# A graph network kernel: each tile of gathered rows fetched once, and copied on the chip to the steps that use it

## What is computed

```python
edge_index = jnp.stack([src, dst])
h = jnp.maximum(_layernorm(x, axis=-1), 0.0)
x = x + _L0_gnn_ref(h, src, dst, L0_gnn_W, L0_gnn_b)              # mean of h[src] over the edges of a node, @ W.T + b
...
x = x + _L1_gnn_ref(h, src, dst, L1_gnn_W_edge, ...)              # mean of relu([h[src], h[dst]] @ W_edge.T), then a linear layer and relu
...
x = x + _L2_gnn_ref(h, edge_index, ...)                           # two graph attention layers, 16 heads of 8
...
x = x + _L3_gnn_ref(h, edge_index, ...)                           # attention by dot products q[dst] * k[src], 2 heads of 64
```

## Time and profile before

| | |
|---|---|
| time, median of 3 runs | 6830.07 us (6825.1 to 6843.93) |
| the profiled execution, its own time | 6823.64 us |
| its span | 6821.9 us |
| mean granted TensorE clock | 0.636 |
| busy shares | PE 49%, PE weight load 42%, DVE 40%, ACT 31%, POOL 50% |
| DMA moved | 564.68 MB, mean 83 GB/s |
| fetches by POOL, L1165 | 3520, busy 3355.5 us |
| chain that ended last, by engine | unknown 48%, DVE 17%, PE 14%, issue 13% |

### The profile page before, as it was taken

The page is one execution under the profiler, slowest core; times in us unless marked ns, Lnnn a source line. Parts: engine busy times, 40 slices in busy tenths (PEclk is TensorE's granted clock), DMA queues, the critical chain, the costliest instruction groups (busy, mean ns, idle before and its releaser), DMA issues.

```text
span 6821.9 us, 113042 instructions
## 1 busy us (share of the span) xinstructions
PE 3345.8 (49%) x30004; PEld 2897.9 (42%) x30005; DVE 2697.0 (40%) x6412; ACT 2103.5 (31%) x6369; POOL 3437.8 (50%) x3641
## 2 busy tenths in 40 slices
PE   1545445444444454454454534444444555555555
PEld 1434334333333343444444534444444455555454
DVE  4222223211111144444444544444445644444445
ACT  1111112222222233444444434444444322222222
POOL 3666664455555525555555355455454444444443
PEclk9565666767776665556555655555666666666666
DMA  4222222222222222222222232222222333333332
GB/s 114 91 87 88 90 85 83 80 74 78 75 76 77 75 56 75 78 78 82 78 78 82 56 83 81 77 78 81 77 77 62 103 97 100 96 98 96 98 95 80
DMA packets 342830, 564.68 MB, mean 83 GB/s; under 512 B 90413, under 2 KB 160957, under 8 KB 342622
## 3 DMA queue, kind: packets, MB, share of 16 engines
q0 software_dynamic: 124288, 289.37, 16.1%
q1 hardware_dynamic: 218354, 273.42, 12.7%
HBM read 490.31 MB, written 72.84 MB: 83 GB/s over the span
## 4 chain that ended last, share of the span: by engine, by line
another core or an unknown queue 48%; DVE 17%; PE 14%; issue 13%; ACT 3%; DVEq 2%; ACTq 1%; POOL 1%; DMA 0%; SPq 0%; POOLq 0%
PE psA L1564 7%; PE psDS L1189 3%; DVE acc L1683 2%; PE psDS L1542 2%; DVE prod L1589 1%; PE psA L1230 1%; DVE lg L1598 1%; DVE seg L1605 1%; DVE lastmax L1615 1%; DVE lastmax L1613 1%; DVE below L1661 1%; DVE V L1670 1%; DVE prod L1396 1%; DVE lastmax L1617 1%
## 5 line engine op out<-in xcount | busy, mean ns | idle before, releaser
L1165 POOL DMA_INDIRECT GT<-table,srcI x3520 | 3355.5, 953 | 3202.6 <-DVE V L1670 1403.7
L1564 PE MATMUL psA<-V,O 128*128 128x144 f32 (+1 forms) x4176 | 988.6, 425 | 10.8 <-ACT psA L1500 5.5
L1189 PE MATMUL psDS<-nodeQ,Ot 128*128 x2816 | 605.7, 390 | 658.3 <-ACT Ot L1181 559.8
L1564 PEld LDWEIGHTS psA<-V,O 128*128 128x128 f32 x4176 | 918.0, 314 | 17.2 <-issue 11.8
L1189 PEld LDWEIGHTS psDS<-nodeQ,Ot 128*128 128x128 f32 x2816 | 544.6, 290 | 696.4 <-issue 691.3
L1519 PE MATMUL psDS<-stageD,Ot 128*128 128x16 bf16 x4224 | 251.4, 173 | 804.2 <-issue 802.9
L1519 PEld LDWEIGHTS psDS<-stageD,Ot 128*128 128x128 bf16 x4224 | 184.3, 102 | 878.2 <-issue 860.4
L1683 DVE TENSOR_TENSOR acc<-acc,psA 128x1296 f32 (+1 forms) x261 | 381.2, 1460 | 413.8 <-remote 349.8
L1661 DVE TENSOR_TENSOR below<-lg,psDS 128x128 f32<-128x128 f32 (+1 forms) x264 | 62.4, 236 | 1157.8 <-remote 1156.6
L1500 ACT COPY psA<-consts 128x1296 f32<-128x1296 f32 (+1 forms) x261 | 315.0, 1207 | 628.4 <-DVE acc L1683 471.9
L1550 PE MATMUL psDS<-newM,Ot 128*128 128x16 bf16 (+1 forms) x6336 | 256.5, 175 | 430.2 <-issue 291.3
(11 more groups left out here) (244 smaller groups left out, 5286.0 us busy)
## 6 DMA issues: line engine op xcount, KB each, us to landing
Ob<-onehots SPq DMA_DIRECT2D x352, 256.0 KB
Ot<-onehots_turned SPq DMA_DIRECT2D x352, 256.0 KB
GT<-table,srcI POOLq DMA_INDIRECT x3520
onehots<-Ob SPq DMA_DIRECT2D x88, 256.0 KB
onehots_turned<-Ot SPq DMA_DIRECT2D x88, 256.0 KB
first<-first_dram SPq DMA_DIRECT2D x176, 64.0 KB
first_dram<-GT SPq DMA_DIRECT2D x18, 384.0 KB, 5.1
table<-nodeQ SPq DMA_DIRECT2D x40, 128.0 KB, 1.9
```

The costliest lines, as they stand in the source:

```text
L1165: eng.indirect_dma_start(out=GT[:, p.k, j, 0:table.shape[1]], out_offset=None, in_=table, in_offset=bass.IndirectOffsetOnAxis(ap=srcI[:, p ...
L1189: ins = eng.matmul(psD[:, j, :], Ot32[:, p.q, j, :], at_block(nodeQ, b[j], D), start=True, stop=True)
L1564: ins = eng.matmul(to, O[:, p.q, j, :], V[:, p.q, j, 0:VW], start=False, stop=j == G - 1, skip_group_check=True)
```

## The change

The first four passes (sum, mlp, gat1, gat2) get their rows in two stages.

- **`fetch_tiles` on POOL** fetches each of the 665 tiles once, in NT = 84 groups of eight, into a ring of 4 x 8 tiles. It is written out, with no hardware loop. From tile group 4 on it first loads from `tiles_over` which step group must have been copied, and waits for that on the new counter `copied`. Behind the fifth fetch of each group it waits for the group before to have landed and raises `landed`. In the gat passes the fourth group also waits for `parted(0)`.
- **`copy_rows` on SP** copies, for each step of a group, its tile from the tile ring to the row ring, which the other engines read as they read `GT` before: it waits for the row ring's release, loads eight slot numbers (`slots_of_steps`) and two needs (`tiles_needed`) into registers, waits for `landed` twice, and issues 4 + 4 DMAs from SBUF to SBUF. `rows_copied` waits for them to land and raises `copied`.
- SP's loads of the next group's one-hot matrices stand between `copy_rows` and `rows_copied` (mlp and gat); in the sum pass both stand ahead of the stores.
- ACT has no `copy_index` in these passes. Both rings share the buffer `rows_of_edges`, whose second part also holds `prod`.
- The setup works out the new index tables: three more loads, one more set of transposes, about ten more vector operations, and a store of the steps' indices to `src_steps`. Some constants move to `Ot32`, and the units begun in the mlp pass move into `acc` (`own_sums`).
- The dot pass keeps `fetch_groups` and `copy_index`; it reads its indices from `srcT`, which SP reloads from `src_steps` at the end of gat2.

The core of the diff, cut:

```diff
-def sweep(eng, n, turn, early=0, late=0):
+def sweep(eng, n, turn, early=0, late=0, tail=0):
...
-    last = (n - early) // RING
+    last = (n - max(early, tail)) // RING
...
-        GT = sb("GT", [P, RING, G, 2 * D])
+        rows_of_edges = sb("rows_of_edges", [P, RING * G * 2 * D + HEADS1 + G * D])
...
+        def fetch_tiles(eng, table, hold=None):
+            tables_stored(eng)
+            to = by_tiles(table.shape[1])[1]
+
+            def has_landed(n):
+                eng.wait_ge(*ring_tiles[n % RING](n // RING, min(G, T - n * G) - 1))
+                eng.sem_inc(landed.sem, 1)
+
+            for n in range(NT):
+                k = n % RING
+                if n >= RING:
+                    eng.wait_ge(*copied(loaded(eng, "over", tiles_over, n - RING, 1, NG - 1, for_waits=True)[0]))
+                    apart(eng)
+                if n == RING - 1 and hold is not None:
+                    eng.wait_ge(*hold(0))
+                for t in range(n * G, min(n * G + G, T)):
+                    eng.indirect_dma_start(
+                        out=to[:, t % (RING * G), :], out_offset=None, in_=table,
+                        in_offset=bass.IndirectOffsetOnAxis(ap=srcT[:, t:t + 1], axis=0),
+                    ).then_inc(ring_tiles[k].sem, 16)
+                    if t % G == G // 2 and n:
+                        has_landed(n - 1)
+            if T % G <= G // 2:
+                has_landed(NT - 2)
+            has_landed(NT - 1)
+
+        def copy_rows(eng, p, w, release):
+            to, of = by_tiles(w)
+            last = isinstance(p.g, int) and p.g == NG - 1
+            eng.wait_ge(*release(p.g - RING))
+            apart(eng)
+            at = loaded(eng, "slots", slots_of_steps, p.g, G, RING * G - 1)
+            need = loaded(eng, "need", tiles_needed, p.g, 2, NT - 1, for_waits=True)
+            parts = [(0, G // 2, need[0]), (G // 2, G, need[1])]
...
+            for a, z, group in parts:
+                eng.wait_ge(*landed(group))
+                apart(eng)
+                for j in range(a, z):
+                    eng.dma_start(to[:, p.k, j, :], of[:, bass.ds(at[j], 1), :].rearrange("p o w -> p (o w)"))\
+                       .then_inc(ring_rows[p.k].sem, 16)
+
+        def rows_copied(eng, p):
+            eng.wait_ge(*ring_rows[p.k](p.i))
+            eng.sem_inc(copied.sem, 1)
...
 # sum pass
-                    fetch_groups(eng, NG, table, sums)
+                    fetch_tiles(eng, table)
...
                     def turn(p):
+                        copy_rows(eng, p, D, sums)
+                        rows_copied(eng, p)
                         eng.wait_ge(*onehot(p.g))
...
-                        if p.has(RING):
-                            copy_index(eng, p.plus(RING))
...
 # mlp pass
-                    sweep(eng, NG, lambda p: load_hots(eng, p, (onehot32,), (turned32,)))
+                    def turn(p):
+                        if p.has(0):
+                            copy_rows(eng, p, D, prodded)
+                        if p.has(1):
+                            load_hots(eng, p.plus(1), (onehot32,), (turned32,))
+                        if p.has(0):
+                            rows_copied(eng, p)
+                    sweep(eng, NG, turn, early=1)
...
 # softmax pass
+                    if gat:
+                        fetch_tiles(eng, table, parted)
+                    else:
+                        fetch_groups(eng, NG, table, values)
...
+                    def turn(p):
+                        if p.has(0):
+                            copy_rows(eng, p, VW, values)
+                        if p.has(1):
+                            load(p.plus(1))
+                        if p.has(0):
+                            rows_copied(eng, p)
...
+                    if to_x == 3:
+                        eng.wait_ge(*landed(NT - 1))
+                        eng.dma_start(srcT[:, :], src_steps).then_inc(src_loaded, 16)
```

More of the change, by code:

```diff
@@ L76, in program @@
     SP_ = SC * P
+    NT = -(-T // G)
     FULL, REST = N // P, N % P
@@ L187, in loaded @@
             eng.load(regs, table[0:1, bass.ds(g * (of or n), n)])
+            if for_waits:
+                if (eng.engine, which, "held") not in reg_sets:
+                    reg_sets[eng.engine, which, "held"] = [eng.alloc_register(f"{which}_held_{j}") for j in range(n)]
+                held = reg_sets[eng.engine, which, "held"]
+                for r, to in zip(regs, held):
+                    eng.reg_alu(to, r, 0, ALU.max)
+                regs = held
             return [eng.snap(r, min_val=0, max_val=most) for r in regs]
@@ L199, in program @@
         noted.per = G
+        ring_tiles = [Count(sem(f"tiles{r}"), G, 16) for r in range(RING)]
+        landed, copied, src_loaded = Count(sem("landed")), Count(sem("copied")), sem("src_loaded")
         ring_rows = [Count(sem(f"rows{r}"), 1, 16 * G) for r in range(RING)]
@@ L370, in _ @@
                     do(eng.tensor_copy, WG[k][:, D:D + 2 * HEADS1], psS[:, 64 * k:64 * k + 2 * HEADS1])
+                eng.wait_ge(tables_turned, TILE_SRC)
+                do(eng.tensor_copy, srcT[:, :], psN[:, 0:SC, :].rearrange("p c s -> p (c s)"))
+                marks["tiles out"] = count
                 eng.wait_ge(fetched, 16 * 2 * SC)
@@ L1171, in copy_index, with tiles_closed @@
+        def rows_copied(eng, p):
+            eng.wait_ge(*ring_rows[p.k](p.i))
+            eng.sem_inc(copied.sem, 1)
+        def tiles_closed():
+            landed.close(NT)
+            copied.close(NG)
+            for k in range(RING):
+                ring_tiles[k].base += 16 * len([t for t in range(T) if t // G % RING == k])
         def copy_index(eng, p):
             if not (isinstance(p.i, int) and p.i <= 0):
-                eng.wait_ge(*ring_rows[p.k](p.i - 1))
+                eng.wait_ge(*ring_tiles[p.k](p.i - 1))
@@ L1346, in _ @@
                     rest_of_units(eng, phase, phase.tensor)
-            close((index, onehot, turned, onehotT, onehot32, sums, counted, added), NG)
+            close((onehot, turned, onehotT, onehot32, sums, counted, added), NG)
+            tiles_closed()
             rows_closed(NG)
@@ L1419, in _ @@
                     rest_of_units(eng, phase, phase.tensor)
-            close((index, onehot32, turned32, toedge, prodded, values, sums, added), NG)
+            close((onehot32, turned32, toedge, prodded, values, sums, added), NG)
+            tiles_closed()
             rows_closed(NG)
@@ L1704, in turn @@
                     def turn(p):
-                        if p.has(RING):
+                        if not gat and p.has(RING):
                             copy_index(eng, p.plus(RING))
@@ L1728, in turn @@
                             act_onehot32(eng, p)
+                    if not gat:
+                        eng.wait_ge(src_loaded, 16)
                     sweep(eng, NG, turn, early=RING, late=1)
```

125 lines of the change are left out of this document (86 added, 39 removed).

## The result

The changed kernel takes 7196.6 us (median of 4 runs, 7184.1 to 7212.5) where the kernel before takes 6828.1: the ratio is 1.0536, with a 95% interval of 1.0509 to 1.0563. The change costs 5.4%. The profiled execution has a span of 7182.4 us against 6821.9. One thing must be known to read what follows: in five of the seven later comparisons the very same kernel before took 4910 to 4920 us (the lower level) and in the other two 6826 and 6832 (the level of this comparison), so kernels are compared only within a level.

What follows compares the result with a forecast made beforehand. It took POOL's fetch stretches, nearly in series with the other engines they slow, as the bound. Fewer fetches −135, starts +45, setup +5, SP's copies +35 gave −50 on 6823.6: 6774, as run median 6780 us; range 6640 to 7500.

Steps and rivals of the forecast that it cites:

- The likeliest case: Whole kernel: fewer fetches outweigh later starts and SP's copies, 6780 us (own range 6690 to 6820), chance 0.36.
- SP becomes the bound: Rival: copy landing not covered, SP's period 14.3 us; sum +220, mlp +53, gats −45 each, 7018 us; chance 0.22.
- P = 14.3: SP's period per group in us if the landing falls outside slow time, in the rival where SP bounds; 0.22.
- signs that were to make the forecast wrong: Sum pass above 12.5 us per group with PE waiting for rows; POOL pauses ending on SP in the gats.
- P = 12.2 us for SP in the sum pass: SP's period per group with copies, landing in slow time; against 11.8 before, +35 us (−49 to +290).
- W: SP's work per group at normal pace, copies, loads, hot matrices and waits: 7.9 us, landing up to 1.9 more.
- s: Time per group in which POOL's fetches slow SP to one instruction per 0.70 us: 4.6 to 6.6 us.
- −45 us for each gat pass: gat1 and gat2: 39 fetches fewer at 1.256 us save 49, 45 counted, taken whole.
- fetches in series with the rest: Gat passes: 10 us of fetches plus some 5 us of free running make the 14.9 us period.
- mlp, −45: mlp pass: the gain from 39 fewer fetches taken whole, since PE suffers there the same way.
- Starts, +45: First four passes: first rows used 22.6 us after the first fetch instead of 11.4, 11.2 later four times.
- The landing of 3.6 us: Copies queued behind fetched rows land in 3.6 instead of 1.9 us; sum-pass period 13.9 us, whole kernel 6930.

Runs made afterwards that it cites:

- e13: Changed kernel with SP counting copies right behind them in mlp and gat, behind the stores in the sum pass; 7217.1 us beside 6825.5 for the kernel before.
- e14: Changed kernel with every second row copy left out (odd steps read old rows); 7185.3 us beside 6825.5 for the kernel before.
- e9: Changed kernel with four of each group's eight copies in the sum pass issued by ACT; 7154.7 us beside 6831.5 for the kernel before.
- e6: Change in the mlp pass alone, sum and both gat passes fetching as before; 6764.0 us beside 6831.5 for the kernel before.
- e16: Changed kernel with POOL in the gat passes also waiting for `values` of the third group behind; 4873.6 us beside 4912.8 for the kernel before.
- e2: Changed kernel with copies counted right behind them in mlp and gat, behind the stores in the sum pass; 5114.8 us beside 4910.0 before.

## Why the prediction was wrong

It forecast 6780 us, faster; measured was slower, 7196.6. The likeliest case was the wrong one of those that it listed. The rival "SP becomes the bound" had the side and the sum pass right (P = 14.3, +220 us) and mlp and the gat passes wrong. Its total is mis-added too: 6830 + 220 + 53 − 90 + 50 is 7063 and not 7018. Both of the signs that were to make the forecast wrong came: a sum pass of over 12.5 us per group with PE waiting for rows, and pauses of POOL that end on SP in the gat passes.

- **The step that failed first: P = 12.2 us for SP in the sum pass**, from a landing that falls into slow time. It doesn't: POOL is released by the count behind the landing, so in 79 of the pass's 88 turns at least nine tenths of the wait for it lay outside of POOL's fetches, and it was added whole, 1.7 us. SP's turn is 14.4 us and the pass +216 us, where the text took +35. The other parts were sized nearly right: W plus landing 7.9 + 1.9 = 9.8 against 10.4 at the lower level, and the slowing 4.0 us of 5.6 x 0.81 = 4.5. But s was taken too narrow: 9.6 us less the 2 to 5 that it names are 4.6 to 7.6 and not 6.6. e13 shows what the landing is worth (119 us of 216) and that the pass is still +110 without it; e14 and e9 show 92 us for half the copies and 57 for moving them to ACT. Whether these gains add wasn't tried; e9 shows another stall by POOL's stretches taking over.
- **The second: −45 us for each gat pass.** They took +101 and +123. The reading of the earlier trace rows, fetches in series with the rest, made the saving whole; it left out that POOL's release would no longer come from V but from SP's count, so that stretches and groups fall out of step. What that costs can be read from the same two profiles, from one `below` of DVE to the next, by how much of POOL's fetching lies between them. Before, 77 of 79 such intervals of gat1 (2600 to 3800 us) have one stretch in them and last 14.8 to 16.0 us. In the changed kernel (2740 to 4020 us) 14 of 77 have none and last 8.4 us (median), 15 have two and last 24.7, so such a pair takes 33.1 us where two groups took 30.0; six have just one and last 14.8 to 18.0, and the rest have parts of stretches. The mean is 16.2 us against 15.0. In e13 (2760 to 4040 us) 36 of 79 have one stretch and last 16.2 us in the median, 13.4 to 18.4. So a stretch of the same length costs the others more at most places than where it fell before. The copies are beside it in all of these intervals, and no run at this level had the old place with copies, so that the place alone is the cause stays argued. Shown is that it isn't SP's number of copies (e14), nor the count behind the loads (e13), nor late rows, nor PE's clock, and that the old form in gat gives the old time (e6).
- **mlp, −45:** right in sign, −85 measured, −68 in e6. It hangs on the count behind the loads: counted ahead of them it is +44 against before (1347 against 1302, e13). 39 fetches of 1.256 us are only 49 us. For the rest there is a term that the text put at nothing, ACT's index copy, since "the ring release sets POOL's start". In mlp it doesn't: before, POOL waited 326 us of the pass for that copy, in 42 of 88 groups, by its list of waits there (below); in the changed kernel 282 us end with SP instead. That this is the missing gain is argued; no run took the copy away alone.
- **Starts, +45:** the first rows are used 18.8 us after the first fetch in the sum pass and 20.8 in mlp (22.6 was said, 11.4 before), by the rows below. Right in kind, 7 and 9 us in place of 11. Setup: +3.8 of +5.
- **The rule of the Trainium skill** (DMA: Bandwidth & Descriptors, "Issuing engines are not separate DMA queues") that a second issuer saves only its sequencer time: e9 moved half of the sum pass's copies to ACT and saved 57 us there, and the trace agrees that the time to be saved is SP's own: the DMA engines had room (21.2% and 14.4% of their time for the two queues, by the page). The landing of 3.6 us that the prediction feared from copies queued behind fetched rows is seen only beside SP's slow pace. In the changed kernel the first store comes 1.7 us behind the copies, and 3.6 (median) in the seven turns in which POOL fetched nearly all the while; at the lower level (e16) it is 1.8 us in the 30 turns with fetches beside it and 1.7 in the seven with none. How much of the 3.6 is the landing and how much SP's own instructions isn't told apart.

```profile
POOL GT L1165 <- ACT srcI L1175: 325.5, 42, 8.2
```

```profile
134.64 3.78 PE L1347 MATMUL psA<-O,rows_of_edges 128*128 128x128 f32 x16 [13.16 <-issue]
```

```profile
1470.85 1.23 DVE L1519 TENSOR_TENSOR rows_of_edges<-psDS,rows_of_edges 128x1024 f32<-128x1024 f32 x1 [15.60 <-DMA rows_of_edges<-rows_of_edges]
```

## What to carry to other kernels

Moving work from the fetching engine to a queue that "has time" needs that queue's whole turn written down, waits for landings included, and compared with the shortest period of any pass that uses it: 9.8 us of work plus 4.0 of slowing against 11.8 us was no margin. A wait can't be hidden in another engine's busy time if it is what lets that engine start. A count that releases the producer belongs where the queue's other work covers the landing, and not ahead of that work (119 us in one pass, 127 in another; nothing in the gat passes). And a change of what releases a producer shifts when its bursts fall; where bursts slow everyone, that alone must be tried pass by pass, since passes answered with opposite signs.

## What was not expected of the hardware

The same kernel takes 6826 to 6832 us in some comparisons and 4910 to 4920 in others; two chips showed both. In the slow ones SP's address operations (FUSED_REGOPS) take up to 0.7 us in the kernel before and up to 1.5 in the changed one (2.1 in e13); of the 152 over 0.3 us in the kernel before, 150 fall beside a fetch of POOL's. In the 13 runs at the lower level none takes more than 0.37 us. Those of SP's copies in the changed kernel, and in e2 at the lower level:

```profile
L1274 SPq FUSED_REGOPS  x2816: 2/55/1533, 127.2 to 5610.2; - x188
```

```profile
L1274 SPq FUSED_REGOPS  x2816: 55/55/95, 127.2 to 4074.4; - x188
```

POOL's fetches take the same 1.256 us in both. At the lower level POOL never pauses in the sum pass of e1 and is the bound. What the two levels come from wasn't found.
